# Neighbour sums: plain rows gathered and multiplied in fp32, a ring of 24, and a wide group's products taken in two halves

## The reference, cut to what matters

```
h_neigh  = feat @ W_neigh
h_sparse = maxk(h_neigh, 32)            # the 32 largest of 256 kept, the rest zero
msg      = h_sparse[src]                # 200,000 edges
summed   = segment_sum(msg, dst, n)
```

## Time and profile before

| | us |
|---|---|
| median of 3 runs | 4519.31 |
| lowest and highest | 4509.97, 4532.03 |
| span of the profiled execution | 5377.8 |
| neighbour sums in it, from the first load to the last product | about 4043 to 4972 |

### The profile page before, as it was taken

How to read it: one execution, slowest core, us unless ns; L and a number is a source line. 1 busy time by engine, 2 the same in 40 slices (tenths; PEclk the granted TensorE clock), 3 DMA queues, 4 the chain that set the end, 5 groups by cost and what they waited for, 6 DMA issues and landing times. The chain is left out here.

```text
span 5377.8 us, 72916 instructions
## 1 busy us (share of the span) xinstructions
PE 3810.4 (71%) x19358; PEld 2805.1 (52%) x19383; DVE 2664.5 (50%) x9403; ACT 1681.8 (31%) x4007; POOL 2947.9 (55%) x2997
## 2 busy tenths in 40 slices
PE   4888886854555555546687777787766788887798
PEld 2455553743333333335565666665525666776566
DVE  7655532543435333325332333333795666666782
ACT  3334443222223222223233333333542222222330
POOL 5777765566666666661554455544165555555121
PEclk9999998977667677765888888888888999999798
DMA  6444444343333333332321222221638888998001
GB/s 220 157 155 149 158 158 145 90 130 88 88 90 88 91 91 90 93 94 30 80 46 41 47 46 47 44 49 37 218 125 287 291 297 301 313 311 286 14 1 48
DMA packets 351400, 690.67 MB, mean 128 GB/s; under 512 B 70225, under 2 KB 173918, under 8 KB 344635
## 3 DMA queue, kind: packets, MB, share of 16 engines
q0 software_dynamic: 139328, 355.39, 22.9%
q1 hardware_dynamic: 211677, 330.60, 18.8%
HBM read 573.39 MB, written 112.35 MB: 128 GB/s over the span
## 5 line engine op out<-in xcount | busy, mean ns | idle before, releaser
L1007 POOL DMA_INDIRECT e_ring<-table,erow x1040 | 1001.5, 963 | 539.2 <-issue 272.4
L1349 PE MATMUL e_sums<-e_ring,e_onehot 128*128 128x257 f32 x2080 | 765.4, 508 | 611.3 <-DVE e_onehot L1262 298.4
L2445 POOL DMA_INDIRECT t_source<-source_rows,t_index x632 | 598.2, 947 | 595.6 <-DVE t_parts L2531 394.8
L1349 PEld LDWEIGHTS e_sums<-e_ring,e_onehot 128*128 128x128 f32 x2080 | 412.5, 238 | 783.4 <-issue 378.3
L1461 POOL DMA_INDIRECT e_ring<-table,esrc x544 | 531.4, 977 | 391.2 <-PE e_sums L1558 239.9
L554 POOL DMA_INDIRECT r_ring<-rows,esrc x528 | 585.8, 1110 | 246.6 <-issue 131.7
L985 ACT ACTIVATE k_sign<-ramp,low 128x128 bf16<-128x128 f32 x1024 | 349.8, 393 | 968.6 <-DMA r_xw<-rows 443.1
L1546 PE MATMUL e_total<-e_loads,e_times 128*128 128x256 f32 x3072 | 519.6, 306 | 1.2 <-issue 1.2
L2640 PE MATMUL t_out<-t_w,t_hidden 128*128 128x256 f32 x1600 | 438.8, 410 | 100.9 <-issue 98.1
L1222 DVE SCALAR_TENSOR_TENSOR big<-e_sums,within,big 128x257 f32 x130 | 62.9, 484 | 826.9 <-remote 666.6
L1444 ACT ACTIVATE e_times<-e_tally 128x320 fp32r<-128x320 f32 (+4 forms) x640 | 255.6, 426 | 668.8 <-PE e_tally L1530 288.8
(11 more groups left out here) (532 smaller groups left out, 6372.0 us busy)
## 6 DMA issues: line engine op xcount, KB each, us to landing
e_loads<-table SPq DMA_DIRECT2D x512, 256.0 KB
table<-r_stage SPq DMA_DIRECT2D x49, 1024.0 KB
outputs<-first_outputs SPq DMA_DIRECT2D x49, 512.0 KB, 6.8
first_outputs<-t_stage SPq DMA_DIRECT2D x96, 256.0 KB
t_near<-near_rows SPq DMA_DIRECT2D x79, 256.0 KB
e_ring<-table,erow POOLq DMA_INDIRECT x1040
table<-n_split SPq DMA_DIRECT2D x49, 256.0 KB
t_source<-source_rows,t_index POOLq DMA_INDIRECT x632
```

Source lines behind the costliest of these rows:

```text
L1007: eng.indirect_dma_start(ring[:, t % RING, 0:D], None, table, bass.IndirectOffsetOnAxis(ap=b.erow[:, EARLY + t:EARLY + t + 1], axis=0)).th ...
L1349: eng.matmul(sums[g % SUMS][:, 0:ACCW], onehot[t % ONEHOTS][:, :], ring[:, t % RING, :], start=(t % GROUP == 0), stop=(t % GROUP == GROUP ...
L2445: eng.indirect_dma_start(source[s][:, q, :], None, a.source_rows, bass.IndirectOffsetOnAxis(ap=index[s][:, q:q + 1], axis=0)).then_inc(gat ...
```

## The change

The gathered part of `neighbour_sums` takes plain rows from `table2`, 1 KB each, into a ring of 24 slots of half the size, and does one fp32 product for each tile where it did two fp32r products. The one-hots of that part are written as fp32. The dense part loads as before from `table3`. TensorE's order is regrouped: for a group with one chunk it is as before; for a group with two, the first chunk of its counts, the first half of the products of the group two back (3 of 5 windows), the second chunk, the other half.

```diff
-    RING = 12
+    RING = 24
...
-        ring = sb("e2_ring", [P, RING, 2, D], F32R)
-        onehot = [sb(f"e2_onehot{s}", [P, P], F32R) for s in range(ONEHOTS)]
+        ring = sb("e2_ring", [P, RING, D])
+        onehot = [sb(f"e2_onehot{s}", [P, P]) for s in range(ONEHOTS)]
...
-                eng.indirect_dma_start(ring[:, t % RING, :, :].rearrange("p n d -> p (n d)").bitcast(F32), None, halves, bass.IndirectOffsetOnAxis(
+                eng.indirect_dma_start(ring[:, t % RING, :], None, table, bass.IndirectOffsetOnAxis(
                     ap=b.esrc[:, FROM + t:FROM + t + 1], axis=0)).then_inc(gathered[t % RING], 16)
...
+            def inner(g, of, to):
+                n = block(g)
+                if of == 0:
+                    if g % COUPLE == 0:
+                        open_totals(g // COUPLE)
+                    eng.wait_ge(copied, units[g + 1])
+                    eng.wait_ge(fetched[g % AHEAD], 16 * (g // AHEAD + 1))
+                for q in range(of, to):
                     for half in range(2):
                         mm = eng.matmul(part(n, q), times[g % TIMES][:, q * P:(q + 1) * P],
                                         loads[:, g % AHEAD, half, :], start=False, stop=False, skip_group_check=True)
-                mm.then_inc(spread, 1)
+                if to == wide(g):
+                    mm.then_inc(spread, 1)
+
+            def group(g):
+                outer(g, 0)
+                if g < 2:
+                    for i in range(1, len(chunks(g))):
+                        outer(g, i)
+                elif len(chunks(g)) == 1:
+                    inner(g - 2, 0, wide(g - 2))
+                else:
+                    half = -(-wide(g - 2) // 2)
+                    inner(g - 2, 0, half)
+                    outer(g, 1)
+                    inner(g - 2, half, wide(g - 2))
...
-                for half in range(2):
-                    mm = eng.matmul(sums[g8 % 2][:, 0:D], onehot[t % ONEHOTS][:, :], ring[:, s, half, :],
-                                    start=(half == 0 and t % GROUP == 0), stop=(half == 1 and t % GROUP == GROUP - 1))
-                mm.then_inc(summed, 1)
+                eng.matmul(sums[g8 % 2][:, 0:D], onehot[t % ONEHOTS][:, :], ring[:, s, :],
+                           start=(t % GROUP == 0), stop=(t % GROUP == GROUP - 1)).then_inc(summed, 1)
```

More of the change, by code:

```diff
@@ L1524, in _, with outer, open_totals @@
         def _(eng):
[L1525 to L1544, removed]
+            def outer(g, i):
+                at, n = chunks(g)[i]
+                u = units[g] + i
+                if i == 0:
+                    eng.wait_ge(marked, 4 * (g + 1))
+                wait_if(eng, copied, u - 1)
+                for two in range(2):
+                    mm = eng.matmul(tally[u % 2][:, 0:n], row[g % (MARKS // 2)][:, two, :],
+                                    place[(2 * g + two) % MARKS][:, at:at + n],
+                                    start=(two == 0), stop=(two == 1))
+                mm.then_inc(tallied, 1)
+            def open_totals(c):
+                wait_if(eng, taken, TAKEN_BY[c])
+                for s in banks[c]:
+                    eng.matmul(total[s][:, :, :].rearrange("p w d -> p (w d)"), zeros[:, 0:P], zeros[:, :],
+                               start=True, stop=False, skip_group_check=True)
+            def inner(g, of, to):
[6 more added lines that the diff above has]
+                for q in range(of, to):
                     for half in range(2):
@@ L1556, in _ @@
                 eng.wait_ge(gathered[s], 16 * (t // RING + 1))
-                for half in range(2):
-                    mm = eng.matmul(sums[g8 % 2][:, 0:D], onehot[t % ONEHOTS][:, :], ring[:, s, half, :],
-                                    start=(half == 0 and t % GROUP == 0), stop=(half == 1 and t % GROUP == GROUP - 1))
-                mm.then_inc(summed, 1)
+                eng.matmul(sums[g8 % 2][:, 0:D], onehot[t % ONEHOTS][:, :], ring[:, s, :],
+                           start=(t % GROUP == 0), stop=(t % GROUP == GROUP - 1)).then_inc(summed, 1)
                 for g in groups_at[t]:
-                    outer(g)
-                    if g > 1:
-                        inner(g - 2)
+                    group(g)
                     if g == GROUPS - 1:
-                        inner(g - 1)
-                        inner(g)
+                        inner(g - 1, 0, wide(g - 1))
+                        inner(g, 0, wide(g))
 def far_edges(nc, b, table, rows, use, reach, targets):
```

## The result

The changed kernel takes 4564.36 us (4555.28 to 4568.33, 4 runs) against 4519.09 us (4509.97 to 4532.03, 4 runs): ratio 1.0096, 95% interval 1.0080 to 1.0112, so about 43 us or 1.0% slower. Forecast: 4559 us.

The account below looks back on a forecast made before the run. Neighbour sums were taken at 749 us, between TensorE's 708 and DMA's bounds; afterwards TensorE needs 708 + 106 - 25 = 789 us, so +40 us gives 4519 + 40 = 4559 us, 0.9% slower, range 4479 to 4615 us.

Parts of the forecast that it names:

- What bounds the kernel: Neighbour sums before: 749 us without recording, between 708 and 829; TensorE 708, GpSimd 680, DMA 716 to 829 us.
- rival C: Neighbour sums: pauses are the kernel's own, TensorE has 218 us of slack; 0 to +30 us, middle 4525 us; chance 0.13.
- rival A: Neighbour sums: TensorE alone set the pace before, DMA cost nothing; +81 us, 4600 us; chance 0.2.
- The product in fp32: Gathered tiles on TensorE: 0.434 us instead of 0.24, 0.194 us a tile, 106 us more; ends 106 and 152.
- The upper price: Gathered tile's fp32 pair on TensorE: 0.52 us behind a short bf16 product, 544 x 0.28 = 152 us more.
- The split: Wide groups' counts: six products between chunks cover the wait for ScalarE's copy, 25 us gained; ends 0 and 48.5.
- TensorE's pace: Neighbour sums before: 5452 matmuls at 0.130 us each, 708 us at the best observed pace.
- Half the gathered bytes: Gathers carry 71.3 instead of 142.6 MB; gains DMA's cost beyond TensorE's 708 us, 41 us, ends 0 to 121.
- The ring: Gather ring of 24 slots: costs and gains nothing, since gathers already come early enough; at most 2 us.
- The signs named: Changed profile: records 0.217 us apart, six products between chunks, `e_tally` ScalarE waits under 10 us, q0 71 MB, longer GpSimd waits.
- Rate 220 GB/s and share below 0.7: DMA engines in the changed neighbour sums: rate falls to about 220 GB/s and busy share below 0.7.
- Short rows and the ceiling of the rate: Gathers: 1 KB rows at 281 GB/s of full share, DMA 656 us, still below TensorE; trace's highest rate 387.

Follow-up runs that it names:

- relief_only: Changed kernel with two fp32r products of each plain 1 KB row instead of one fp32 product, old order of chunks, ring of 24: 4471.68 us, ratio 0.9901 against the kernel before.
- fp32_only: Changed kernel with both chunks of a wide group's counts one after the other as before: 4567.44 us, ratio 1.0109 against the kernel before.
- quarter_plain: Kernel before with every fourth gathered tile (136 of 544) as plain 1 KB rows and one fp32 product: 4504.67 us, ratio 0.9965.
- ring12: Changed kernel with 12 slots in the ring for 24: 4575.63 us, ratio 1.0117 against the kernel before.
- split_only: Kernel before with only TensorE's group order of the change: 4516.57 us, ratio 1.0001.
- quarter_split: quarter_plain with the change's order of wide groups: 4502.85 us, ratio 0.9959 against the kernel before.
- half_plain: Kernel before with every second gathered tile (272 of 544) as plain rows and one fp32 product: 4526.06 us, ratio 1.0014.
- before_again: Kernel before, unedited, for a second profile: span 4516.2 us, ratio 1.0002.
- loads_deeper: Kernel before with 12 slots for loads and 8 for gathers in place of 8 and 12: 4521.27 us, ratio 1.0003.
- heavy_gather: fp32_only with 2 KB rows gathered into a ring of 12, the second half of each not multiplied: 4575.16 us, ratio 1.0121 against the kernel before.
- one_product: Changed kernel with one fp32r product of the plain rows for each tile instead of the fp32 one: 4474.27 us, ratio 0.9898 against the kernel before.

## Why the prediction was right

**What bounds the kernel.** The disturbed profile showed TensorE waiting for marks and copies and never for data. Both readings that followed from the waits alone would have been wrong: that TensorE has 218 us of slack (rival C), and that DMA is hidden (rival A). Taking the sum of work and the bounds from the stretches at full pace, instead of the waits, gave 749 us for the stage, and it is 749.8. In part that is luck: it was a middle between 716 and 781, and the 781 rested on shrinking a disturbed stage like the whole. The reason that holds is the DMA rate with full queues, 387 GB/s in the earlier trace rows, which is the plateau of the undisturbed kernel (I had called it a window in which TensorE pauses; it was busy 4.41 of 5 us there). The 33 us above 717 come from the dips, which I had no row for.

**The product in fp32.** Forecast 0.194 us a tile, 106 us. The timeline shows it, 0.43 against 0.24 us. Over the whole stage a plain tile costs less, 0.17 us, by the pairs of kernels that differ in nothing else of weight: 92.3 us from relief_only to fp32_only, 70.7 from quarter_plain to ring12 for the other three quarters of the tiles. So the term was right in kind and 13 us too large; why the timeline's difference doesn't add up in full is open. The upper price (0.52 us behind a short bf16 product) did not occur.

**The split.** Forecast 25 us, measured 0: 796.1 against 796.2 us of stage, and no gain in two other pairs (split_only, quarter_split). This is the term that failed, the largest error of the sum. It was taken as half of 48.5 us of waits of the weight loads, most of which sat beside pauses that do not exist without the disturbance; the real number is 13 us, and not even these were on the path, since they are idle time of the weight load and not of the matmuls (1.2 us). The timeline had said 14 us and I went above it.

**TensorE's pace.** 708 us at the best observed pace, and 708 by the mixed kernels with the ring of 12, taken back to no plain tile. Taken on to all tiles, quarter_plain and half_plain give 731.0 + 3 x 23 = 800 us, and ring12 has 801.7.

**Half the gathered bytes.** 41 us forecast. The stage of relief_only is 45.9 us shorter, 41 without the part of the ring. It ends at GpSimd's 702 to 704 us, which happen to lie where TensorE's own need with the ring of 24 also lies, so a second limit that I had put at 680 us was as near as the first.

**The ring.** Forecast 0, measured 5 us of gain at the end of the stage. I had looked at the waits in the middle, where there are none.

**Why the sum came out.** 708 + 106 - 25 = 789 was the forecast of the stage. The runs give 708 + 93 - 0 - 5 = 796. The errors of 13, of 25 and of 5 us have different signs, and leave 7. That the mechanism is right (a stage of DMA becomes one of TensorE, by the fp32 product) is shown; that the total is met within 5 us is luck.

**The signs named.** Pair of records 0.217 us apart: yes, 0.216. Six products between the chunks: yes. ScalarE's share in the waits of `e_tally` under 10 us: yes, 0.4, though it was 13.0 and not 48.5 before. TensorE's pace falls by 80 us of work or more: yes, by 93. q0 at 71 MB: yes. GpSimd waits longer for slots than before: yes, 117.0 against 83.0 us. Rate 220 GB/s and share below 0.7: no, 260 and 0.85. The rate was an error of mine, 205.6 MB over the old 929 us. The share was forecast as if it fell with the bytes. It doesn't: the short rows ran at 71.34 / (0.318 x 802) = 280 GB/s of their full share, as the relation sums had said, where the long ones of the second profile ran at 373; and the loads, unchanged, at 322 where they had 361.

**Short rows and the ceiling of the rate.** The Trainium skill (Perfetto Trace Analysis, "DMA Optimizations") says that transfers under 2 KB carry a significant overhead each. A gather here is one transfer of 128 rows; read on its rows, the trace agrees, 280 GB/s of a full share for rows of 1 KB against 373 for rows of 2 KB. The Trainium skill (DMA: Bandwidth & Descriptors, "Bandwidth") has 425 GB/s for a lone core, by which the result would have been +81, an estimate. The trace doesn't agree: in 40 slices of this stage none of the runs passes 389.

## What to carry to other kernels

Where one engine's work is traded for bytes, work out both full-pace times and compare them: here 750 us of DMA (717 without its dips) against 708 of TensorE. Moving all tiles put 93 us on TensorE and overshot; moving a quarter of them put 23 on it and gained. A profile whose span is far above the runs is a disturbed one: distrust its waits, sum the work, and take rates from the stretches in which the queue was full. A wait of the weight load cost here only what the matmuls themselves stood idle. A share of DMA near 1 doesn't say that DMA sets the pace: change the bytes and see. And look at the end of a stage by itself: where the work of one kind runs out, the depth of the other's buffer counts.

## What the runs showed of the hardware

- The DMA engines stand at 386 to 387 GB/s when 2 KB gathers and 256 KB loads run together (before_again, loads_deeper). With 1 KB gathers in place of the 2 KB ones they are busy 0.91 of the time at 295 GB/s (relief_only).
- The busy share of the DMA engines doesn't follow the bytes: with the same 277 MB it is 1.01 at 370 GB/s in before_again, and in the middle of heavy_gather, where TensorE sets the pace, 0.98 at 350.
- A 128x128 by 128x256 product of one fp32r matmul holds TensorE 0.12 us, an fp32 one 0.43 us as two records of 0.216 us. Exchanging two fp32r for one fp32 costs 0.17 us a tile over the stage.
- In one execution of the same kernel TensorE's signals reached the other engines 1.5 to 3 us after its recorded work, and the whole took 862 us longer than in the second profile. The cause stays open.
- GpSimd issues a gather every 1.25 us at best, with rows of 1 KB and of 2 KB, and every 1.29 us on average where nothing holds it (relief_only, one_product): 702 to 704 us for the 544 of this stage.
